# Quantized attention: 26 row norms as ScalarE activations with a scale and a bias per row, the bias made by GpSimd

## The reference

```python
def _layernorm(x, axis=-1, eps=1e-05):
    m = jnp.mean(x, axis=axis, keepdims=True)
    v = jnp.var(x, axis=axis, keepdims=True)
    return (x - m) / jnp.sqrt(v + eps)
...
    x = x + _L1_attn_ref(_layernorm(x, axis=-1), L1_attn_Wq, ...)
    x = x + _L1_xattn_ref(_layernorm(x, axis=-1), ctx_2048, L1_xattn_Wq, ...)
    x = x + _L1_ffn_ref(_layernorm(x, axis=-1), L1_ffn_w_router, ...)
```

```python
    q = jnp.transpose(q * scale, (0, 2, 1, 3))
    q = _fq_sym(q, axis=-1)          # rounded to 127 steps of its largest value
    k = _fq_sym(k, axis=-1)
    v = _fq_sym(v, axis=2)
    attn = jnp.einsum('bhqd,bhkd->bhqk', q, k)
    attn = jax.nn.softmax(attn.astype(jnp.float32), axis=-1)
    attn = _fq_unsigned(attn, axis=-1)   # rounded to 255 steps of the row's largest
    out = jnp.einsum('bhqk,bhkd->bhqd', attn, v)
```

## Time and profile before

| | |
|---|---|
| median of 3 runs | 1383.9 us (1382.39 to 1384.28) |
| device time of the profiled execution | 1390.76 us |
| its span | 1388.7 us |
| busy over the span | PE 82%, DVE 65%, ACT 46%, POOL 42% |
| the quantized attention's rounds | from 812 to 1140 us of the span |

### The profile page before, as it was taken

The page is one execution under the profiler, slowest core; times in us unless marked ns, Lnnn a source line. Parts: engine busy times, 40 slices in busy tenths (PEclk is TensorE's granted clock), DMA queues, the critical chain, the costliest instruction groups (busy, mean ns, idle before and its releaser), DMA issues.

```text
span 1388.7 us, 24766 instructions
## 1 busy us (share of the span) xinstructions
PE 1145.3 (82%) x7640; PEld 812.3 (58%) x7679; DVE 895.9 (65%) x2497; ACT 632.9 (46%) x1432; POOL 583.2 (42%) x890
## 2 busy tenths in 40 slices
PE   3699989982999999657888767787787778999988
PEld 2577757772566666445665535565565555688855
DVE  5576764664332222347977479999999974665557
ACT  3164653330311111214644459888898871433300
POOL 6143543346311111133646434465566654355510
PEclk9799999996999999867989779988988889999999
DMA  5866735013111111164552030000000003455454
GB/s 141 199 197 160 189 105 182 29 39 97 51 46 47 46 47 46 54 173 114 140 135 57 2 125 2 1 33 17 25 25 32 33 33 129 117 162 158 152 177 145
DMA packets 75534, 127.10 MB, mean 92 GB/s; under 512 B 11624, under 2 KB 58792, under 8 KB 71912
## 3 DMA queue, kind: packets, MB, share of 16 engines
q1 hardware_dynamic: 61870, 95.13, 25.3%
q0 software_dynamic: 10272, 28.39, 5.6%
q10 hardware_dynamic: 3264, 2.01, 0.5%
HBM read 76.97 MB, written 48.13 MB: 90 GB/s over the span
## 4 chain that ended last, share of the span: by engine, by line
PE 53%; issue 12%; POOL 11%; ACT 8%; DVE 7%; DMA 5%; ACTq 1%; SPq 1%; POOLq 0%; DVEq 0%
PE ps L1147 15%; PE ps L228 15%; PE ps L1164 7%; ACT work L1884 5%; POOL work L1918 4%; PE ps L477 3%; POOL xs_scratch L1478 3%; DMA W<-work 2%; PE ps L1132 2%; PE ps L1156 2%; PE ps L459 1%; PE ps L300 1%; PE ps L490 1%; DVE work L594 1%; DMA W<-q_parts 1%
## 5 line engine op out<-in xcount | busy, mean ns | idle before, releaser
L1147 PE MATMUL ps<-W,work 128*128 x628 | 227.5, 495 | 1.5 <-issue 1.4
L1884 ACT ACTIVATE work<-ps,work 128x512 f32<-128x512 f32 x256 | 205.0, 821 | 40.3 <-POOL work L1918 39.2
L1496 POOL DMA_INDIRECT ys_scratch<-work x118 | 113.1, 959 | 259.0 <-DVE work L1340 113.2
L594 DVE TENSOR_REDUCE work<-ps 128x2 f32<-128x512 f32 (+1 forms) x192 | 127.7, 685 | 85.5 <-PE ps L459 83.9
L1822 DVE TENSOR_REDUCE work<-ps 128x1 f32<-128x512 f32 x256 | 172.8, 681 | 15.1 <-PE ps L1729 9.8
L1390 DVE TENSOR_TENSOR work<-work,ps 128x128 f32<-128x128 f32 (+1 forms) x118 | 49.7, 422 | 200.6 <-ACT work L1459 200.3
L766 POOL TENSOR_SCALAR_AFFINE_SELECT work<-work 128x256 f32<-128x256 f32 (+1 forms) x192 | 92.6, 485 | 166.8 <-ACT work L700 165.7
L1918 POOL TENSOR_SCALAR work<-work 128x1 f32<-128x1 f32 x256 | 100.0, 390 | 126.4 <-DVE work L1822 113.0
L1147 PEld LDWEIGHTS ps<-W,work 128*128 128x128 f32 x628 | 111.0, 192 | 68.6 <-issue 62.4
L700 ACT ACTIVATE work<-ps 128x512 f32<-128x512 f32 x192 | 110.6, 598 | 74.1 <-PE ps L477 73.8
L1164 PE MATMUL ps<-W,work 128*128 x470 | 121.1, 381 | 0.0
(11 more groups left out here) (260 smaller groups left out, 2367.8 us busy)
## 6 DMA issues: line engine op xcount, KB each, us to landing
work<-xs_scratch SPq DMA_DIRECT2D x79, 132.0 KB, 2.2
W<-ys_scratch SPq DMA_DIRECT2D x16, 512.0 KB, 3.9
q_parts<-work SPq DMA_DIRECT2D x48, 128.0 KB, 1.8
W<-q_parts SPq DMA_DIRECT2D x16, 384.0 KB
W<-in_w_in SPq DMA_DIRECT2D x6, 1024.0 KB, 11.4
work<-xs_scratch SPq DMA_DIRECT2D x39, 130.0 KB, 2.1
W<-k_parts SPq DMA_DIRECT2D x8, 512.0 KB
W<-q_parts SPq DMA_DIRECT2D x16, 256.0 KB
```

Of the source, the lines that this page charges most:

```text
L594: q.e.tensor_reduce(self.m[:, j, h0:h0 + n], ov, AX, ALU.max).then_inc(*up("mx", L, b, u))
L1147: mm = q.e.matmul(PS[bks[c]][:, 0:N], self.XT[s % 2][:, k, :], w[:, k, bass.ds(regs[s] + 512 * c if c else regs[s], N)], start=k == 0, sto ...
L1496: q.e.indirect_dma_start(YS[L], bass.IndirectOffsetOnAxis(ap=self.dst[n % self.NY], axis=0), self.YB[n % self.NY], None).then_inc(*landing ...
L1884: q.e.activation(self.ee[n // 2 % 3][:, 512 * (h % 2):512 * (h % 2) + 512], PS[banks.of["c1_s", t, h]][:, :], ACT.Exp, bias=self.nb[:, h:h ...
```

## The change

All 26 norms that stand beside the rounds of the quantized attention leave VectorE. Their places in the programs are these:

- GpSimd makes -mean * rstd for both tiles of a pair, one 128x1 instruction each, into the two columns of `ve` (`ln_bias`): for stage 5 in round 11, between line 1918's instruction and that of line 1934, for stage 4 in round 13.
- ScalarE computes x * rstd + that bias with one activation (Identity) per tile (`act_norm1`): for stage 5 in rounds 12 and 13, the second ahead of the copy at line 1879, for stage 4 in rounds 14 and 15.
- Who reads a normed tile now waits for ScalarE's event `xna` where ScalarE made it (`xn_at`).

```diff
+        def xn_at(s, t):
+
+            return at("xna" if s == 4 and t > 3 or s == 5 and t < 14 else "xn", s, t)
...
+        def ln_bias(q, s, p):
+
+            q.wait_ge(at("rstd", s, p))
+            for t in (2 * p, 2 * p + 1):
+                q.e.tensor_scalar(ve[:, t:t + 1], mv[:, t, 0:1], rstd[:, t:t + 1], -1.0, ALU.mult, ALU.mult).then_inc(*up("nmr", s, t))
+
+        def act_norm1(q, s, t, base=()):
+            if s not in (2, 5):
+                before = ln_before.get((s, t // 2))
+                q.wait_ge(at("ln_t", *before) if before else None)
+            q.wait_ge(at("nmr", s, t), *base)
+            q.e.activation(normed(s, t), x[:, t, :], ACT.Identity, bias=ve[:, t:t + 1], scale=rstd[:, t:t + 1]).then_inc(*up("xna", s, t))
...
-                    if h in (14, 15) and self.ln4(t):
-                        ln_norm1(q, 4, 2 * self.ln4(t) + h - 14)
...
-                    if h in (11, 12) and self.ln5(t) is not None:
-                        ln_norm1(q, 5, 2 * self.ln5(t) + h - 11, ends(4))
...
+                    if h in (14, 15) and self.ln4(t):
+                        act_norm1(q, 4, 2 * self.ln4(t) + h - 14)
+                    if h in (12, 13) and self.ln5(t) is not None:
+                        act_norm1(q, 5, 2 * self.ln5(t) + h - 12, ends(4))
                     if h == 13 and t + 1 < T:
                         self.act_q3T(q, t + 1)
...
+                    if h == 11 and self.ln5(t) is not None:
+                        ln_bias(q, 5, self.ln5(t))
+                    if h == 13 and self.ln4(t):
+                        ln_bias(q, 4, self.ln4(t))
                     if h == 10 and self.ln5(t) is not None:
                         ln_pow(q, 5, self.ln5(t))
```

More of the change, by code:

```diff
@@ L297, in ln_turn @@
             for j in (0, 1):
-                q.wait_ge(at("xn", s, 2 * p + j))
+                q.wait_ge(xn_at(s, 2 * p + j))
                 for k in (0, 1):
@@ L781, in pool_fin1 @@
                     t = 2 * b + j
-                    q.wait_ge(at("On", 1, b, j), at("x_e", 0, t, 1), at("xn", 3, t))
+                    q.wait_ge(at("On", 1, b, j), at("x_e", 0, t, 1), xn_at(3, t))
                     q.e.tensor_tensor(x[:, t, :], x[:, t, :], self.On[j], ALU.add).then_inc(*up("x_a1", t))
@@ L786, in pool_fin2 @@
                 t = 2 * b + j
-                q.wait_ge(*x_ready(0, t), at("w_o0", "b"), at("xn", 0, t))
+                q.wait_ge(*x_ready(0, t), at("w_o0", "b"), xn_at(0, t))
                 q.e.tensor_tensor(x[:, t, :], x[:, t, :], b_o0, ALU.add).then_inc(*up("xa0", t))
@@ L1024, in vector @@
                         t, bk, o = 2 * b + j, banks.of["c0pv", b], 8 * j + 16 * (b % 2)
-                        q.wait_ge(at("c0_pv", b), at("xn", 1, t), done)
+                        q.wait_ge(at("c0_pv", b), xn_at(1, t), done)
                         e.scalar_tensor_tensor(out=x[:, t, :], in0=PS[bk][:, 256 * j:256 * j + 256], scalar=sm[:, o + 3:o + 4],
@@ L1411, in dve_shared @@
                     t = 4 * blk + i
-                    q.wait_ge(at("sh_o", t), at("xn", 5, t), at("x_e", 1, t, 3) if t >= 12 else None)
+                    q.wait_ge(at("sh_o", t), xn_at(5, t), at("x_e", 1, t, 3) if t >= 12 else None)
                     q.e.scalar_tensor_tensor(out=x[:, t, :], in0=PS[banks.of["sh_o", t]][:, 0:256], scalar=0.2, in1=x[:, t, :],
@@ L1418, in add @@
                 L, K = self.L, self.K
-                q.wait_ge(at(f"ld{t % 4}", 2 + L, t), at("x_b0", t) if L == 0 else at("x_s", t) if t < 12 else at("xn", 5, t))
+                q.wait_ge(at(f"ld{t % 4}", 2 + L, t), at("x_b0", t) if L == 0 else at("x_s", t) if t < 12 else xn_at(5, t))
                 for j in range(K):
@@ L1476, in pool_scatter @@
                     for j in range(K):
-                        q.wait_ge(at("idx", L, p), at("xn", self.ln, t))
+                        q.wait_ge(at("idx", L, p), xn_at(self.ln, t))
                         q.e.indirect_dma_start(XS[L], bass.IndirectOffsetOnAxis(ap=self.idx[:, t, j:j + 1], axis=0),
@@ L1491, in gpsimd @@
                     for t in range(T):
-                        q.wait_ge(at("x_c0", t), at("w_xa", "r"), at("xn", 2, t))
+                        q.wait_ge(at("x_c0", t), at("w_xa", "r"), xn_at(2, t))
                         q.e.tensor_tensor(x[:, t, :], x[:, t, :], b_m0, ALU.add).then_inc(*up("x_b0", t))
@@ L1932, in gpsimd @@
                     if h == 11 and t < T:
-                        q.wait_ge(at("x_a1", t), at("w_cr1", "bp"), at("xn", 4, t))
+                        q.wait_ge(at("x_a1", t), at("w_cr1", "bp"), xn_at(4, t))
                         q.e.tensor_tensor(x[:, t, :], x[:, t, :], bp1, ALU.add).then_inc(*up("c1_xb", t))
```

## The result

The changed kernel takes 1398.2 us against 1384.1 (medians of four runs each); the ratio is 1.0094, 95% interval 1.0062 to 1.0126. That is slower, by 13.0 us by the ratio (8.6 to 17.4 by its interval), where 7.6 were forecast.

What follows compares the result with a forecast made beforehand. It took the ring through GpSimd and ScalarE, not VectorE, to bound the odd tiles; 3.9 + 1.1 + 0.7 + 0.3 + 1.6 = 7.6 us slower, 1383.9 + 7.6 = 1391.5 us for the median, range 1379 to 1397.5.

Steps and rivals of the forecast that it cites:

- The ring through GpSimd and ScalarE: Attention rounds: maximum, bias, exponential, scores, maximum, with four banks of slack; claimed late on GpSimd and ScalarE; chance 0.48.
- VectorE's 98%: Rival in the stage: VectorE's queue, 98% busy, is the bound; 10.6 us come off, 1373.3, or 1378.6 with half; faster 0.20.
- Tile 13: Sign before the change: no stage 4 statistics and norms, VectorE busy 10.27 us instead of 12.34, yet the stretch takes 12.74.
- Removed norms: 26 norms off VectorE, 10.6 us of its time: worth nothing on the path in tiles 5 to 15, 0.3 us in tile 3.
- GpSimd's pair: Two added 128x1 bias instructions on GpSimd, 0.7 us a pair; the stage 5 pair counted on the path in full.
- heavier on GpSimd: Rival: VectorE's roundings fall on GpSimd's queue at other moments, 0.44 x 2 more in seven tiles; 13.6 us, 1397.5; chance 0.13.
- ScalarE's norms: 26 added 128x256 activations on ScalarE: pitch 0.35 us each, bounds 0.25 and 0.68; the first stage 5 one free.
- the two paths of 1.05 and 1.6: Tiles 5, 7, 11: growth of 1.05 us through TensorE, 1.6 through head 15's exponential; loss between them, taken 1.3.
- the slack of the even rounds: Behind the odd tile's late stretch: may take up part of ScalarE's delay, so 1.3 us was taken.
- the rounding in 3': VectorE's rounding in round 3 of the next tile; from the odd tile's round 10 to it 13.5 to 14.2 us, not 12.55.
- The stage 4 pair as covered by ScalarE: GpSimd's stage 4 biases delay heads 13 to 15 by 0.7 us, counted as covered because ScalarE is late by more.
- Even tiles: The tiles between the odd ones: should be unchanged after the change.

Runs made afterwards that it cites:

- short norms: Against the kernel before: the 26 norms still on VectorE, but over 16 of 256 columns, nothing added beside the rounds; ratio 1.0039, stage 335.2 us.
- stage 4 norms in the even tile: Against the changed kernel: stage 5 norms back on VectorE, stage 4 norms on ScalarE one tile later, in round 8; ratio 1.0045, stage 335.6 us.
- the biases alone: Against the changed kernel: norms back on VectorE, GpSimd still makes the 26 biases but nobody uses them; ratio 1.0093, stage 342.6 us.

## Why the prediction was right or wrong

- **What bounds the stage.** Right. The ring through GpSimd and ScalarE, and not VectorE's 98%, sets the odd tiles: two kernels that only took work off VectorE there (short norms, stage 4 norms in the even tile) lengthened them by 0.6 to 0.7 us (tile 9 by 0.4). Tile 13, where VectorE had less to do and was no faster, was the right sign.
- **Removed norms.** Taken as worth nothing in tiles 5 to 15. There is no single price: shortening them in the kernel before costs 0.7 us in each of tiles 5, 7 and 11 and 0.4 in tile 9, while putting them back beside the change costs 0.3 in each and 2.9 in the stage. It depends on where the rounding then falls. VectorE's busy time over the stage fell from 310.6 to 303.4 us, by 7.2 and not by the 12.9 that I had said, and its waits for scores grew by 18.7.
- **GpSimd's pair.** Taken as 0.7 us on the path; the pitch of two was 0.45. But I had weighed collisions as a rival of 0.13 only, and one is in tiles 5, 7, 9 and 11: head 11's bias meets the rounding, 0.33 us. The sum of both, 0.78, is near the 0.7 by luck, for a reason I did not have.
- **The rival "heavier on GpSimd".** Its 13.6 us are nearer to the measured 13.0 than my 7.6, and its time of 1397.5, the top of my range, nearer to the 1396.9 that the ratio gives. Its mechanism came true only in part: roundings do meet GpSimd's instructions at other moments, but the residual's bias, which it priced, takes 0.72 to 0.73 us in every tile of the changed kernel, and what is drawn out on the path is 0.33 in tile 7, not 0.88. Most of the rest is ScalarE's.
- **ScalarE's norms.** The mis-sized term. I took a pitch of 0.35 from the Identity that reads PSUM; this one, from and to the on-chip memory with a scale and a bias from memory, has a record of 0.59 to 0.62 (forecast 0.45 to 0.6) and a pitch of 0.49. Three times 0.14 is 0.4 us a tile.
- **How much of it counts.** I took 1.3 between the two paths of 1.05 and 1.6, "as a part of ScalarE's delay may meet the slack of the even rounds". It met none in tiles 5 to 11: the 1.98 us of head 15 came through whole, and the stretch to the rounding in 3' took 14.55 us where I had said 13.5 to 14.2. With 0.49 in the sum and the full path the forecast for tile 7 would have been 0.7 + 3 x 0.49 - 0.15 = 2.0.
- **The stage 4 pair as covered by ScalarE.** Right in the full change, where ScalarE is late by more; wrong without it, as the biases alone showed.
- **Even tiles.** Forecast unchanged, measured +3.0 us, 1.6 of them in tile 2. Of the 1.6 more than 1 us is not there in the two other executions of the same code (20.57 and 20.21 against 20.02 before), though tile 1 is longer in them (20.29 and 20.49 against 19.88). I did not find out why the rest came; even tiles lie near 20.2 or near 20.75 in several of the kernels.

So 2.5 us net were missing in the odd tiles and the end, and 3.0 in the even ones; with them 7.6 becomes 13.1. The 2.5 are in the main the larger pitch and the full path; the 3.0 are open.

## What to carry to other kernels

An engine that is 98% busy need not be the bound: look for a place where it already has less work (here tile 13) and see whether that place is shorter. In this ring an instruction on the "idle" engine cost its full pitch where that engine was the late one (0.45 us for the pair of biases, 0.49 for a norm), so place such work by the timeline, in front of the wait and not behind it. Where VectorE and GpSimd work side by side, a small shift of either can move one under the other (0.43 us between two starts against 0.44 here): compare the records of one repeated small instruction before and after.

## What the runs showed of the hardware that I had not expected

- A 128x1 tensor_scalar on GpSimd is drawn out from 0.26 to 0.53 to 0.59 us, and a pair from 0.61 to 0.88 to 1.23, when VectorE's tensor_scalar of 128x1024 from float32 to bfloat16 starts beside it. For a pair 0.44 us from its start to that of the rounding is enough to avoid it, 0.43 is not. By the Trainium skill, page SBUF — State Buffer, section Who interferes with whom, VectorE in a two-port mode and GpSimd lock each other out for a whole instruction. The trace agrees in kind: 0.27 to 0.62 us are added, up to nearly the rounding's whole 0.68; in which mode the rounding runs, no trace here shows.
- The stage starts between 799.2 and 809.4 us in the profiled executions of the ten kernels whose code is the same up to there. Spans of whole kernels can hide 8 us of a change, as they did here; in the stretch that it touches about 1 us is uncertain.
